# Recurrent heads in f32: four heads per weight array instead of two, tanh read straight from PSUM, and the spreading of the inputs moved to GpSimd

## The reference

```python
x = tokens * rsqrt(mean(tokens ** 2) + 1e-4) * norm_w      # (B, T, 16, 8)
a_t = tanh(a)                                              # (16, 64, 64)
for t in range(T):
    state = tanh(einsum('bhs,hst->bht', state, a_t) + einsum('bhd,hds->bhs', x[t], b))
    mixed[t] = einsum('bhs,hsd->bhd', state, c) + skip * x[t]
out = tokens + mixed.reshape(B, T, 128) @ w_out.T + b_out
```

## Time and profile before

| what | value |
|---|---|
| median of 3 runs | 3547.36 us (3545.41 to 3551.08) |
| span of the profiled execution | 3541.9 us |
| the stage's opening, 807.2 to 827.2 us | 20.0 us |
| its 512 steps, 827.2 to 1475.4 us | 648.2 us |
| its tail, 1475.4 to 1487.1 us | 11.7 us |
| instructions | 57755 |

### The profile page before, as it was taken

One profiled execution on the slowest core, in us unless ns is written; L12 is line 12 of the kernel. 1 busy time (PEld: TensorE's weight loads), 2 busy tenths in 40 slices (PEclk: granted clock), 3 DMA queues, 4 the chain that ended last, 5 costly groups with the idle time before them and its releaser, 6 DMA issues. The chain is left out here.

```text
span 3541.9 us, 57755 instructions
## 1 busy us (share of the span) xinstructions
PE 3172.6 (90%) x21270; PEld 1680.4 (47%) x21277; DVE 2204.9 (62%) x5867; ACT 1780.1 (50%) x4015; POOL 1035.8 (29%) x454
## 2 busy tenths in 40 slices
PE   8888899997888888898989898988889898999998
PEld 3333344445777777643433343333334344556447
DVE  5777445446666666666478702889980166963991
ACT  3555423424444444426377524777752455753762
POOL 1111100000000000000089501999960103960990
PEclk8999999996555555699989999999999999999999
DMA  5443331120000000030400000000000200231124
GB/s 149 108 104 89 97 93 41 56 78 25 3 3 3 3 3 3 2 98 1 170 0 1 0 0 0 1 1 1 0 1 0 87 1 21 87 155 72 71 96 178
DMA packets 76776, 168.46 MB, mean 48 GB/s; under 512 B 9552, under 2 KB 46544, under 8 KB 67920
## 3 DMA queue, kind: packets, MB, share of 16 engines
q1 hardware_dynamic: 76496, 164.78, 14.2%
HBM read 120.70 MB, written 44.04 MB: 47 GB/s over the span
## 5 line engine op out<-in xcount | busy, mean ns | idle before, releaser
L1249 PE MATMUL psum<-h_ring,h_parts 128*128 128x4 bf16 (+2 forms) x12288 | 418.0, 170 | 121.3 <-ACT h_ring L1337 121.3
L2273 DVE TENSOR_TENSOR_SCAN s_hh<-psum,s_dbu 128x512 f32<-128x512 f32 x384 | 445.5, 1207 | 41.0 <-ACT psum L2098 39.6
L2185 POOL TENSOR_TENSOR s_dbu<-s_du,s_bb 128x1024 f32<-128x1024 f32 x190 | 443.0, 2358 | 43.8 <-ACT s_bb L2081 43.8
L1249 PEld LDWEIGHTS psum<-h_ring,h_parts 128*128 128x128 bf16 x12288 | 372.3, 105 | 171.1 <-ACT h_ring L1337 145.0
L1959 PE MATMUL psum<-s_term,w_c 128*128 128x512 f32 x768 | 405.8, 616 | 4.2 <-POOL s_term L2192 4.2
L1337 ACT ACTIVATE h_ring<-h_pre 128x16 f32<-128x16 f32 x1024 | 168.3, 211 | 357.6 <-DVE h_pre L1399 357.6
L2098 ACT ACTIVATE psum<-s_delta,s_decay 128x512 f32<-128x512 f32 x384 | 261.6, 690 | 65.8 <-DVE s_hh L2273 65.5
L901 POOL MEMSET r_weights<- 128x512 f32 x4 | 2.1, 525 | 930.1 <-POOLq L1222 660.5
L910 DVE TENSOR_TENSOR f_hid<-f_gate,psum 128x512 f32<-128x512 f32 x184 | 126.6, 688 | 204.8 <-PE psum L836 198.0
L1399 DVE TENSOR_REDUCE h_pre<-psum 128x16 f32<-128x48 f32 x1024 | 165.0, 203 | 141.7 <-PE psum L1249 141.7
L897 ACT ACTIVATE f_gate<-psum 128x512 f32<-128x512 f32 x184 | 109.7, 597 | 281.6 <-PE psum L832 281.4
(11 more groups left out here) (495 smaller groups left out, 6380.0 us busy)
## 6 DMA issues: line engine op xcount, KB each, us to landing
x_spill<-x_flip SPq DMA_DIRECT2D x28, 1024.0 KB, 3.8
f_share<-f_wide SPq DMA_DIRECT2D x208, 128.0 KB, 3.0
a_ks<-a_spread SPq DMA_DIRECT2D x96, 128.0 KB, 3.3
a_qs<-a_spread SPq DMA_DIRECT2D x96, 128.0 KB, 3.9
x_spare<-x_spill SPq DMA_DIRECT2D x4, 2048.0 KB, 7.7
x_raw<-x_spill SPq DMA_DIRECT2D x4, 2048.0 KB, 7.6
x_norm<-x_spill SPq DMA_DIRECT2D x4, 2048.0 KB, 7.6
w_l3f<-in_l3f SPq DMA_DIRECT2D x1, 7240.0 KB, 21.2
```

Source lines behind the costliest of these rows:

```text
L1249: mm = nc.tensor.matmul(columns_of(s // BLOCK, grp)[:, s % BLOCK, 0:3 - part, cols], parts[:, part, GROUP * grp + p, :], upper[:, (s - 1) ...
L2185: nc.gpsimd.tensor_tensor(dbu[:, s % D_RING], du[:, t % 2], both(bb[:, s % B_RING, :]), ALU.mult).then_inc(dbu_ready, 1)
L2273: nc.vector.tensor_tensor_scan(hh[:, s % 4, half, :], DECAYS[i % 3], dbu[:, s % D_RING, half, :], 0.0, ALU.mult, ALU.add).then_inc(scan_do ...
```

## The change

Four heads now share one weight array, as four 64x64 blocks in its quadrants (`at`, built once for even and once for odd steps with the two middle heads exchanged). A moving operand has 16 columns, four heads times four batch entries, and only half of each product is wanted; the places of the wanted halves alternate between even and odd steps. There are two groups of two arrays, so a step has 4 matmuls, in f32, without remainders. ACT reads the wanted halves straight out of PSUM with tanh, one instruction for partitions 0 to 63 and one for 64 to 127, per group. DVE no longer stands in the chain; it copies the states of each block into `hist` (4 copies) and, now inside the steps, adds the inputs, mixes and adds the output for each span of 128 steps. GpSimd spreads the inputs of all 64 blocks. Laying is two matmuls of 256 columns per block (before 128), mixing four f32 matmuls of 64 columns per block (before two of 128), and the projection is made by spans of 128 steps.

The core of the diff:

```diff
-                def add_part(part, s, grp):
-                    for p in range(GROUP):
-                        cols = slice(BATCH * p, BATCH * p + BATCH)
-                        mm = nc.tensor.matmul(columns_of(s // BLOCK, grp)[:, s % BLOCK, 0:3 - part, cols],
-                                              parts[:, part, GROUP * grp + p, :], upper[:, (s - 1) % TURN, grp, 0:3 - part, cols],
-                                              start=False, stop=True, skip_group_check=True)
-                    return mm
+                def advance(i, grp):
+                    for q in range(GROUP):
+                        cols = slice(q * 4 * BATCH, (q + 1) * 4 * BATCH)
+                        mm = nc.tensor.matmul(columns_of(i // BLOCK, grp)[:, i % BLOCK, cols], at[:, i % 2, GROUP * grp + q, :],
+                                              ring[:, (i - 1) % TURN, grp, cols], start=False, stop=True, skip_group_check=True)
+                    mm.then_inc(drive[grp], 1)
...
+                    if s in (2, 3) and blk + 1 < BLOCKS:
+                        lay_inputs(blk + 1, s - 2)
+                    if piece and place in MIX_AT:
+                        mix_in(piece - 1, MIX_AT.index(place))
+                    if i % SPAN == SPAN // 2 and i > SPAN:
+                        project_out(i // SPAN - 1)
                     for grp in range(2):
-                        pe.wait_ge(state[grp], n)
-                        add_part(2, s, grp)
-                    for grp in range(2):
-                        pe.wait_ge(rest[grp], n)
-                        add_part(1, s, grp)
-                    for grp in range(2):
-                        pe.wait_ge(last[grp], n)
-                        add_part(0, s, grp).then_inc(drive[grp], 1)
...
+                        if i:
+                            pe.wait_ge(state[grp], 2 * i)
+                        advance(i, grp)
...
+                for n in range(4 * PAIRS):
+                    mix_in(TIME // PIECE - 1, n)
...
-                        act.wait_ge(summed[grp], n)
-                        nc.scalar.activation(ring[:, (n - 1) % TURN, grp, 0, :], pre[:, grp, :], ACT.Tanh).then_inc(state[grp], 1)
+                        act.wait_ge(drive[grp], i + 1)
+                        for half in range(2):
+                            rows = slice(S * half, S * half + S)
+                            nc.scalar.activation(valid(ring[rows, i % TURN, grp, :], i % 2, half),
+                                                 valid(columns_of(blk, grp)[rows, s, :], i % 2, half), ACT.Tanh).then_inc(state[grp], 1)
...
-                def sum_up(s, grp, n):
-                def cut_first(s, grp, n):
-                def cut_second(s, grp, n):
```

More of the change, by code:

```diff
@@ L1187, in recurrent_heads @@
     nc, bank, w = g.nc, g.bank, g.w["l1a"]
-    PAIRS, S, BLOCK = 8, 64, 8
-    GROUP = PAIRS // 2
-    WIDTH = GROUP * BATCH
+    HEADS, QUADS, S, BLOCK = 16, 4, 64, 8
+    GROUP = QUADS // 2
+    COLS = GROUP * 4 * BATCH
     TURN = 2 * BLOCK
[L1192 to L1203, removed]
+    BLOCKS, SPAN, PIECE = TIME // BLOCK, 128, 32
+    PAIRS = GROUP * 2
+    MIX_AT = tuple(s for s in range(PIECE) if s % BLOCK >= 4)
+    with stage(g, InnerNorm.SEMAPHORES + " weights_bounded squared ms_ready logged rms_ready x_ready cleared "
+                  "laid_free laid drive0 drive1 state0 state1 kept mix_ready mix_kept out_ready biased resid_done") as (sb, sems):
+        (weights_bounded, squared, ms_ready, logged, rms_ready, x_ready, cleared,
+         laid_free, laid, drive0, drive1, state0, state1, kept, mix_ready, mix_kept, out_ready, biased, resid_done) = sems[6:]
+        drive, state = (drive0, drive1), (state0, state1)
+        at = sb("h_at", [P, 2, QUADS, P])
         sq = sb("h_sq", [P, TOKENS])
@@ new lines, in mix_in @@
+                def mix_in(piece, n):
+                    if n == 0:
+                        pe.wait_ge(kept, (piece + 1) * PIECE // BLOCK)
+                    parity, p = n // (2 * PAIRS), n % (2 * PAIRS)
+                    first, per = piece * PIECE, SPAN // PIECE
+                    home = bank[4 + piece // per % 2].rearrange("p (t b) -> p t b", b=BATCH)
+                    if n == 0 and piece % per == 0 and piece >= 2 * per:
+                        pe.wait_ge(resid_done, piece // per - 1)
+                    mm = nc.tensor.matmul(home[:, piece % per * PIECE + parity:(piece % per + 1) * PIECE:2, :],
+                                          w["c"][:, (parity * 2 * PAIRS + p) * P:(parity * 2 * PAIRS + p + 1) * P],
+                                          hist[:, first + parity:first + PIECE:2, p // PAIRS, p % PAIRS * BATCH:(p % PAIRS + 1) * BATCH],
+                                          start=(p == 0), stop=(p == 2 * PAIRS - 1))
+                    if n == 4 * PAIRS - 1:
+                        mm.then_inc(mix_ready, 1)
@@ new lines, in project_out @@
+                def project_out(c):
+                    pe.wait_ge(mix_kept, c + 1)
+                    nc.tensor.matmul(bank[4 + c % 2].rearrange("p (b t) -> p b t", b=BATCH), w["out"],
+                                     mix[:, :, c * SPAN:(c + 1) * SPAN], start=True, stop=True).then_inc(out_ready, 1)
+                pe.wait_ge(rms_ready, CHUNKS)
+                for grp in range(2):
+                    lay_inputs(0, grp)
+                pe.wait_ge(weights_bounded, 1)
+                pe.wait_ge(cleared, 1)
@@ L1274, in _ @@
+                for i in range(TIME):
+                    blk, s = divmod(i, BLOCK)
+                    piece, place = divmod(i, PIECE)
+                    if s in (2, 3) and blk + 1 < BLOCKS:
+                        lay_inputs(blk + 1, s - 2)
                     if piece and place in MIX_AT:
                         mix_in(piece - 1, MIX_AT.index(place))
+                    if i % SPAN == SPAN // 2 and i > SPAN:
+                        project_out(i // SPAN - 1)
                     for grp in range(2):
-                        pe.wait_ge(state[grp], n)
@@ L1289, in _ @@
-                pe.wait_ge(mix_kept, TIME // SPAN)
-                for j in range(CHUNKS):
-                    nc.tensor.matmul(bank[j][:, :], w["out"], mix[:, j, :], start=True, stop=True).then_inc(out_ready, 1)
+                        if i:
+                            pe.wait_ge(state[grp], 2 * i)
+                        advance(i, grp)
+                warm(nc, g, bank[7], 4)
+                for n in range(4 * PAIRS):
+                    mix_in(TIME // PIECE - 1, n)
+                warm(nc, g, bank[7], 4)
@@ L1420, in add_input, with keep @@
-                def add_input(j):
-                    nc.vector.tensor_tensor(fixed(g.resid, j), fixed(g.resid, j), fixed(g.normed, j), ALU.add).then_inc(biased, 1)
-                for c in range(TIME // SPAN):
+                def add_input(j):
+                    nc.vector.scalar_tensor_tensor(out=fixed(g.resid, j), in0=fixed(g.normed, j), scalar=w["b_out"],
+                                                   in1=fixed(g.resid, j), op0=ALU.add, op1=ALU.add).then_inc(biased, 1)
+                def keep(blk):
+                    for grp in range(2):
+                        dve.wait_ge(state[grp], 2 * (blk + 1) * BLOCK)
+                    first = blk % 2 * BLOCK
+                    for parity in range(2):
+                        for half in range(2):
+                            rows = slice(S * half, S * half + S)
+                            src = ring[rows, first + parity:first + BLOCK:2, :, :].rearrange("p t g c -> p t (g c)")
+                            dst = hist[rows, blk * BLOCK + parity:(blk + 1) * BLOCK:2, :, :].rearrange("p t g c -> p t (g c)")
+                            if parity == 0:
+                                src = src.rearrange("p t (k u b) -> p t k u b", u=2, b=BATCH)[:, :, :, half, :]
+                                dst = dst.rearrange("p t (k b) -> p t k b", b=BATCH)
+                            else:
+                                src = src.rearrange("p t (q v c) -> p t q v c", q=QUADS, v=2)[:, :, :, half, :]
+                                dst = dst.rearrange("p t (q c) -> p t q c", q=QUADS)
+                            done = nc.vector.tensor_copy(dst, src)
+                    done.then_inc(kept, 1)
@@ L3244, in weight_parts, with turned @@
     n = "L1_attn_a_"
[L3245 to L3250 removed]
+    quads = [[4 * q + k for k in range(4)] for q in range(4)]
+    def turned(q, parity):
+        h0, h1, h2, h3 = quads[q]
+        return (h0, h1, h2, h3) if parity == 0 else (h0, h2, h1, h3)
+    c_own = np.concatenate([blocks((P, P), [(0, 8 * low, a[n + "c"][low]), (64, 8 * high, a[n + "c"][high])])
+                            for parity in range(2) for q in range(4)
+                            for low, high in ((lambda t: ((t[0], t[1]), (t[2], t[3])))(turned(q, parity)))], axis=1)
+    a_four = np.concatenate([blocks((P, P), [(64 * (k // 2), 64 * (k % 2), a[n + "a"][h]) for k, h in enumerate(turned(q, parity))])
```

(3 more changed lines are left out.)

132 lines of the change are left out of this document (44 added, 88 removed).

## The result

The changed kernel takes 3988.02 us (median of 4 runs, 3980.85 to 3992.34) where the kernel before took 3549.22 in the same session: ratio 1.1234, 95% interval 1.1217 to 1.1251, slower. The forecast was 3996 us in a range of 3940 to 4070.

The account below looks back on a forecast made before the run. The prediction took the steps to be bound by PE's f32 weight loads at the half clock: steps +444, opening +2, tail +3, so +449 on a span of 3541.9, plus 5.5, gives 3996 us, range 3940 to 4070.

Parts of the forecast that it names:

- The price of an f32 load: In PE's small f32 matmuls, each record takes 0.214 us at the half clock and 0.111 at full clock.
- The steps' sum: Over the 512 steps, loads, laying, mixing and projection make 1092 us in place of 648.2, +444.
- The clock: Through all steps PE's granted clock stays at half, 0.50, as in the kernel before.
- Rival 1: In the steps, f32 loads cost 0.11 us each and the chain binds: 3487 us in all; chance 6%.
- Waits don't break PE's list: In the steps PE queues loads over satisfied waits, so no group pays 0.12 us for its first load's start.
- rival 2: PE cannot queue over waits, so steps pay 0.25 us more, +126: 4124 us in all; chance 6%.
- the ring: A step's loop from product through tanh to the next product; forecast as hidden behind the loads, costing 0.
- The chain: From a group's last load slot through two tanh to its next load: 0.67 us, hidden behind 0.86 of loads.
- Cover lost: Laying and mixing, before hidden in PE's waits of 0.5 us a step, now cost 108 and 103 us.
- Opening and tail: Before and after the steps: opening +2 us, tail +3, with about 2 for a next stage opening at half clock.
- Hidden work: DVE's, GpSimd's and ACT's work in the steps runs beside 17 us of PE a block and costs nothing.
- rival 3: The clock comes and goes, lifted a quarter of the time in the steps: 3872 us in all; chance 5%.

Follow-up runs that it names:

- a_bf16: Changed kernel with the recurrence's weights in bf16 and only the upper half of each state read by the product: 3382.95 us, ratio 0.9536 to the kernel before.
- a_half: Changed kernel with one of the two matmuls of each group and step: 3585.12 us, ratio 1.0112 to the kernel before.
- q_parts3: Changed kernel's arrays, tanh and GpSimd spreading, but the product from three bf16 parts, lists ordered by part: 3712.39 us, ratio 1.0481 to the kernel before.
- a_warm2: Changed kernel with two bf16 filler matmuls of 512 columns in each step and 20 ahead of the first: 4310.81 us, ratio 1.2151 to the kernel before.
- a_onetanh: Changed kernel with one tanh per group and step in place of two: 3986.25 us, ratio 1.1234 to the kernel before.
- a_thinmix: Changed kernel with 4 of the 16 mixing matmuls of each piece inside the steps: 3903.08 us, ratio 1.1002 to the kernel before.
- b_thinmix: Kernel before the change with 2 of the 8 mixing matmuls of each piece inside the steps: 3545.01 us, ratio 1.0003 to the kernel before.
- a_actput: Changed kernel with the spreading of the inputs back on ACT from the third block on: 3988.25 us, ratio 1.1247 to the kernel before.

## Why the prediction was right

- **The price of an f32 load** (0.214 us at the half clock) is the step on which everything hung. 4096 loads of 333 ns, four a group in 0.85 us, confirm it; a_bf16 and a_half show it by taking loads away. The steps' sum was 1092 us, measured 1089.2. What these runs price is a load with its matmul; that the load and not the columns sets the slot is read from its being the same 0.213 us with 16 columns and, in mixing (0.427 for two records), with 64. The rule of the Trainium skill that fast weight load is not for FP32 ("TensorE: Matmul & The Clock Gate", Weight-path perf modes) agrees with all runs: loads of the same array are 0.03 us apart in bf16 (q_parts3: 24 in the time of 3.5 f32 ones) and 0.213 in f32.
- **The clock**: 0.50 through all steps, as said. The prediction had it by likeness, from the steps before and from three of four router bursts, and not from a mechanism; the run bore it out, and no run tells why. Rival 1 (loads of 0.11) had the price at the full clock right, 0.112 a record in a_warm2; the chip didn't grant that clock. The rule of the Trainium skill that a load takes columns / 1.2 ns (the same page, LDWEIGHTS), which is given there without a clock, makes 0.107: near the f32 slot at the full clock, 0.112, and half of the 0.213 at the half clock.
- **Waits don't break PE's list** (rival 2): loads follow each other 0.213 apart over all waits; a_onetanh confirms that the ring isn't on the path.
- **The chain**: forecast 0.67 us behind a group's last slot with 0.19 to spare. Measured: tanh 0.27 after the slot's end and 0.38 for the pair; with the forecast's hop of 0.06 that is 0.71, 0.15 to spare. The pair was mis-sized (0.33 taken), without effect, since the loads cover it. a_half, where they don't, came out at the sum made with 0.38.
- **Cover lost**: laying and mixing were to cost 108 and 103 us. Steps of 2.56 and 2.13 us against 1.71 are 0.85 and 0.42 each, 108 and 102 us in all; a_thinmix and b_thinmix show the two sides.
- **Opening and tail**: the opening was to add 2 us and added 0.9. The tail's +3 was 1.1 of its own, measured 1.5, and 2 for a next stage that opens at the half clock. This last term was wrong: behind the stage the granted clock is 1.00, and the work is as fast as before. After and before:

```profile
1928.41:1933.30 4.89, 4.85 (x11) 2.12 (x12) 0.40 (x1) 4.23 (x7) 0.52 (x1) 1.00 0.00 0
1487.10:1492.00 4.90, 4.87 (x11) 2.12 (x12) 0.42 (x1) 4.24 (x7) 0.53 (x1) 1.00 0.00 2
```

- **Hidden work**: DVE 64 us and GpSimd 76 us in 1089; a_actput adds ACT's.

Three slips changed nothing. The clock is at 5 or 6 tenths in eight slices of the earlier trace rows and not in seven; rival 2's sum is 4122 us and rival 3's 3870, each 2 us off.

The medians differ by 439 where the sum was 449. Of these 10 us the steps are 3, the opening 1 and the next stage's clock 2; the other 4 are within the scatter of the runs.

## What to carry to other kernels

Price a small matmul by its weight load, in the type and at the clock that the stage is really granted: with 16 columns the load is the whole cost, and at the half clock an f32 one counts as seven in bf16, and each f32 matmul has two, so that 4 f32 matmuls were dearer than 24 bf16 ones with their remainders. A shorter list of instructions and an emptier VectorE say nothing if the engine in the ring pays more; and work that was free in its waits must be added to the bill when the waits go. With two groups in one in-order list, write out which group's wait stands ahead of which matmul before counting them as overlapped.

## What the runs showed of the hardware

- Four tanh on 64 partitions and 16 elements, from PSUM, start 0.20 us apart, busy 178 ns each; two on 128 partitions from SBUF took 0.33 us together, busy 211 ns each. Two halves, 0.38 us, are dearer than one whole; the source differs as well, and no run separates the two.
- The f32 loads of the recurrence start 0.112 us apart at the full clock (a_warm2, 870.94 to 871.50 us) and 0.213 at the half clock. Behind a pair of wide bf16 matmuls (870.40 to 870.99 us) the first of them, at 870.62 us, runs under the pair. That fits two fillers at the half clock lengthening a plain step by 0.67 us and not by 0.85.
- With two fillers of 512 columns in each step the granted clock was 1.00 for 57 us and then 0.50, with PE shown busy throughout; in the kernel before, with one or two, it was 0.51 from 840 us on. Whether more of them would keep it at 1.00 wasn't tried. A plain step of 1.24 us in place of 1.71 would be a gain on the changed kernel, but my own estimate for that clock in all steps, 3695 us, is still above the kernel before.
